# Modulated 1D convolutions (four layers, one core): the blurred taps of layer 1 are made before layer 0's first products

## The reference, cut to what matters

```python
def _layer(x, style, w, b, mw, mb, typ):
    s = style @ mw.T + mb
    weight = SCALE * w * s[:, None, :, None]
    demod = lax.rsqrt(jnp.sum(weight * weight, axis=(2, 3)) + EPS)
    weight = weight * demod[:, :, None, None]
    if typ == 'same':
        out = jax.vmap(_conv_same)(x, weight) + b[None, :, None]
    elif typ == 'upsample':
        out = jax.vmap(_conv_up)(x, weight.transpose(0, 2, 1, 3)) + b[None, :, None]
        out = _blur(out, 2.0 * blur_k, (1, 1))
    elif typ == 'downsample':
        xb = _blur(x, blur_k, (2, 2))
        out = jax.vmap(_conv_down)(xb, weight) + b[None, :, None]
    return out
out = x
for i, typ in enumerate(('same', 'upsample', 'same', 'downsample')):
    out = _layer(out, style, weights[i], biases[i], mod_w[i], mod_b[i], typ)
x = x + out
```

## Time and profile before

| | before |
|---|---|
| median of 3 runs | 181.14 us (180.51 to 181.2) |
| the profiled execution | 181.34 us, span in the trace 179.2 us |
| granted TensorE clock, mean over the span | 0.98 |
| PE (matmul) busy | 170.8 us, 95% |
| VectorE busy | 125.4 us, 70% |
| ScalarE busy | 57.2 us, 32% |
| GpSimd busy | 15.4 us, 9% |
| chain that ended last | PE 91%, DVE 3%, issue 2%, ACT 1% |

### The profile page before, as it was taken

The page is one execution under the profiler, slowest core; times in us unless marked ns, Lnnn a source line. Parts: engine busy times, 40 slices in busy tenths (PEclk is TensorE's granted clock), DMA queues, the critical chain, the costliest instruction groups (busy, mean ns, idle before and its releaser), DMA issues.

```text
span 179.2 us, 7986 instructions
## 1 busy us (share of the span) xinstructions
PE 170.8 (95%) x3567; PEld 155.4 (87%) x3567; DVE 125.4 (70%) x265; ACT 57.2 (32%) x126; POOL 15.4 (9%) x47
## 2 busy tenths in 40 slices
PE   7899999999999799999999999999999999999990
PEld 5598969986677498999999999999999999998960
DVE  7659755896776946758494949494949394958793
ACT  3433554122142233324151514243332424222110
POOL 7002202800001300200000000000000000000000
PEclk9958999999999999999999999999999999999999
DMA  4960003033000986827274645456463637333322
GB/s 135 365 75 2 4 0 91 4 89 123 0 5 4 273 278 240 225 88 222 98 170 161 159 166 152 177 115 214 103 224 91 237 89 236 93 121 75 140 117 117
DMA packets 11778, 23.65 MB, mean 132 GB/s; under 512 B 5184, under 2 KB 5728, under 8 KB 11744
## 3 DMA queue, kind: packets, MB, share of 16 engines
q1 hardware_dynamic: 11680, 23.12, 42.8%
q10 hardware_dynamic: 64, 0.02, 0.1%
HBM read 8.85 MB, written 8.39 MB: 96 GB/s over the span
## 4 chain that ended last, share of the span: by engine, by line
PE 91%; DVE 3%; issue 2%; ACT 1%; DVEq 0%
PE p_m L415 26%; PE p_le L354 14%; PE p_lo L354 13%; PE p_le L398 12%; PE p_m L433 11%; PE p_lo L385 5%; PE p_le L304 2%; PE p_m L294 1%; PE p_le L402 1%; PE p_m L512 1%; PE p_m L505 1%; DVE r_sb L769 1%; PE p_m L285 1%; PE p_m L343 1%; PE p_m L495 1%
## 5 line engine op out<-in xcount | busy, mean ns | idle before, releaser
L415 PE MATMUL p_m<-u,Hw 64*64 64x256 f32 x896 | 61.0, 377 | 0.3 <-DVE z_sb L787 0.3
L415 PEld LDWEIGHTS p_m<-u,Hw 64*64 64x64 f32 x896 | 46.9, 132 | 2.6 <-issue 0.5
L354 PE MATMUL p_lo<-xin,w0s 64*64 64x259 f32 x384 | 31.0, 406 | 0.0
L736 DVE SCALAR_TENSOR_TENSOR Hw<-p_le,pvec,Hw 128x320 f32<-128x320 f32 x16 | 8.8, 551 | 31.0 <-ACT Hw L605 31.0
L354 PE MATMUL p_le<-xin,w0s 64*64 64x260 f32 x384 | 30.1, 407 | 0.2 <-DVE Hw L743 0.2
L398 PE MATMUL p_le<-R_sb,F_st 64*64 64x192 f32 x320 | 30.0, 324 | 0.0
L398 PEld LDWEIGHTS p_le<-R_sb,F_st 64*64 64x64 f32 x320 | 25.8, 133 | 1.1 <-issue 0.4
L354 PEld LDWEIGHTS p_lo<-xin,w0s 64*64 64x64 f32 x384 | 21.8, 137 | 2.4 <-issue 0.3
L354 PEld LDWEIGHTS p_le<-xin,w0s 64*64 64x64 f32 x384 | 20.7, 137 | 3.4 <-issue 1.1
L605 ACT ACTIVATE Hw<-p_le,pvec 128x448 f32<-128x448 f32 x16 | 10.2, 635 | 37.0 <-PE p_le L398 37.0
L787 DVE SCALAR_TENSOR_TENSOR z_sb<-p_m,pvec,s_sb 128x512 f32<-128x512 f32 (+1 forms) x30 | 21.0, 742 | 0.9 <-PE p_m L415 0.9
(11 more groups left out here) (122 smaller groups left out, 155.9 us busy)
## 6 DMA issues: line engine op xcount, KB each, us to landing
xin<-in_x_dram SPq DMA_DIRECT2D x16, 512.0 KB, 4.8
out_dram<-ot SPq DMA_DIRECT2D x16, 512.0 KB, 5.4
Hw<-Hw SPq DMA_DIRECT2D x30, 192.0 KB, 3.0
wn<-in_L_cond_weights_dram SPq DMA_DIRECT2D x1, 192.0 KB, 3.5
mwn<-in_L_cond_mod_w_dram SPq DMA_DIRECT2D x1, 128.0 KB, 2.3
xe<-in_x_dram SPq DMA_DIRECT2D x2, 56.0 KB, 8.2
cn<-in_cond_dram ACTq DMA_DIRECT2D x1, 16.0 KB, 2.1
bn<-in_L_cond_mod_b_dram ACTq DMA_DIRECT2D x1, 1.0 KB
```

The lines of the kernel that those rows point to most:

```text
L354: ins = pe.matmul(bank[h * C:(h + 1) * C, s, 0:n], w0s[p % 2][rows, k, :], xin[p % NX][rows, i0:i0 + 2 * n - 1:2], start=(k == 0), stop=(k ...
L415: ins = pe.matmul(bank(h)[s * C:(s + 1) * C], tap(p, h, s, blk), u[p % 2][h * C:(h + 1) * C, s, j, k:k + NM], start=(k == 0), stop=(k == l ...
```

## The change

The taps are no longer made after `compose_R(0)`. The two matmuls of k = 0 are issued on TensorE ahead of the demodulation products, the four of k = 1 and 2 right behind them, both ahead of layer 0 of pair 0. They now go to `p_le[:, 0]` instead of `p_m2[:, 1]`. Since layer 0's even products write to the same bank, these wait until ScalarE has copied the taps out. ScalarE makes that copy ahead of `evac_odd(0)` instead of behind `evac_R(0)`. Where the taps stood, TensorE now waits for the copy `G_mv` and for `dt_` before layer 2's taps.

```diff
-            def blurred_taps(l, bank, cid, n):
+            def blurred_taps(l, bank, cid, n, taps=range(K)):
-                for k in range(K):
+                for k in taps:
                     for h in range(2):
...
             ins.then_inc(put["GT"], 1)
 
+            pe.wait_ge(made["cid"], 1)
+            blurred_taps(1, p_le[:, 0], cid2, NF, (0,))
+
             pe.wait_ge(copied["wsumT"], 1)
             pe.wait_ge(made["style2"], 1)
...
             ins.then_inc(put["demod"], 1)
+            blurred_taps(1, p_le[:, 0], cid2, NF, (1, 2)).then_inc(put["FT"], 1)
...
             layer0_odd(0)
+            pe.wait_ge(copied["F_st"], 1)
             layer0(0, p_le, NE, 0, le_done)
             pe.wait_ge(copied["V_st"], 1)
             compose_R(0)
 
-            pe.wait_ge(made["cid"], 1)
+            pe.wait_ge(copied["G_mv"], 1)
             pe.wait_ge(made["dt"], 1)
-            blurred_taps(1, p_m2[:, 1], cid2, NF).then_inc(put["FT"], 1)
             taps_transposed(2, b_m13[0], 256).then_inc(put["w2T"], 1)
...
             act.activation(dq[:], dt_[:], ACT.Sqrt).then_inc(sqrt_done, 1)
+            act.wait_ge(put["FT"], 1)
+            act.activation(F_st[:], p_le[:, 0, 0:NF * C].rearrange("p (a c) -> p a c", c=C), ACT.Copy,
+                           scale=1.0 / 32).then_inc(copied["F_st"], 1)
             evac_odd(0)
...
             evac_R(0)
-            act.wait_ge(put["FT"], 1)
-            act.activation(F_st[:], p_m2[:, 1, 0:NF * C].rearrange("p (a c) -> p a c", c=C), ACT.Copy,
-                           scale=1.0 / 32).then_inc(copied["F_st"], 1)
             make_A(1)
```

## The result

| | before | changed |
|---|---|---|
| first series, median of 6 executions each | 181.15 us (180.51 to 181.25) | 183.14 us (181.17 to 183.22) |
| ratio, with 95% interval | | 1.0079 (1.0043 to 1.0115) |
| second series, median | 181.63 us (31 executions) | 181.99 us (10), ratio 1.0023 (0.9985 to 1.006) |
| profiled execution | 181.34 us, span 179.2 | 181.17 us, span 179.0 |

The change made the kernel slower in the first series, and by an amount that can't be told from nothing in the second. The places at which TensorE's granted clock falls and rises differ from one execution to the next (in four traces of the changed kernel the rise lies between 14.6 and about 16.5), and the time follows them. Over all 18 executions of the change the median is 182.26 us and 8 are at 182.6 or more. Of 90 of the kernel before one is at 182.6 or more, and three more are at 182.51 to 182.53.

A forecast was written before the change was run, and what follows sets the result against it. TensorE's work was taken as the bound (busy 95%), with 1.01 us of VectorE slack in the prologue. An earlier clock rise gains 0.95 to 1.05 us, less 0.1 for later tight spots: 0.9, so 180.3 us, range 179.9 to 181.7.

The forecast's parts named there:

- Which t: Prologue, TensorE: long matmuls from 8.43 us bring the clock's rise, t, earlier; gain 0.9 us, chance 0.45.
- before 13 us: Sign of a right forecast: TensorE's granted clock in the prologue rises before 13 us.
- 8.98 + t/2: Layer 0 of pair 0, TensorE: its end in us, t being the clock's rise; 16.54 for t = 15.12.
- t unchanged: Prologue, clock rise still at 15.12 us: `make_diffs(0)` starts at 16.65, 1.25 late; H(1) 0.1 late.
- cap by VectorE: VectorE needs 4.50 us from `make_diffs(0)` to the sum of H(0)'s taps; gain capped at 0.95 to 1.05.
- A: Rival, chance 0.38: prologue clock rises where it did, VectorE takes TensorE's gain; 181.2 us, range 180.9 to 181.5.
- B: Rival, chance 0.13: prologue clock rises later, at 17.6 us, as taps may not count like layer 0's matmuls; 182.6 us.
- C: Rival, chance 0.04: prologue clock does not stay down at 8.30 us or comes back at once; 179.7 us.
- forecast 0.36, bounds 0.2 and 0.5: Demodulation products on TensorE, behind the two early taps matmuls: late by 0.36 us, moving `dt_` from 10.19 to 10.55.
- The wait of layer 0's even products for `F_st`: TensorE, layer 0: costs nothing, as the odd products hide the 0.44 us copy; uncovered it would be 0.7 us.
- GpSimd's start does not move: `xse` beside VectorE's `pvec` instructions: starts unchanged, so part of VectorE's 0.36 us delay is absorbed; 0.2 taken.

The follow-up runs named there:

- filled kernel: The change with a dummy matmul on the other 64 array rows beside each taps matmul: medians 180.14 us (ratio 0.9944) and 180.91 us (0.9973).
- third alone: Kernel before with only the two k = 0 taps matmuls moved ahead of the demodulation products: median 180.90 us, ratio 0.9966.
- none ahead: The change with all six taps matmuls behind the demodulation products: median 183.09 us, ratio 1.0081 against the kernel before.

## Why the prediction was wrong, point by point

Forecast was 180.3 us, faster by 0.5%; measured was 183.14 in the first series, outside of 179.9 to 181.7, and slower.

**The step that failed is "Which t".** I took the taps for long matmuls like layer 0's, and concluded from "long matmuls (320 columns) from 8.43 on" that the clock would rise earlier. It did not: the low stretch stayed 6.8 us long in three traces of the change with a fall, with rises at 14.6, 15.2 and 16.3, and in the one without a fall the low rate lasted until about 16.5; "before 13 us" was forecast. What the text had as a point for rivals, that the taps use 64 of 128 rows, is what the filled kernel points to: with the other rows busy beside them the stretch was 3.4 us. I had named that reason and weighed it as a detail. Nothing in between was seen either: of the ten traces with a fall ahead of layer 0's end, seven have a low stretch of 6.8 us and three one of 3.4.

**What hangs on t was right.** The rule for layer 0's end, 8.98 + t/2, can be held against the traces: for rises at 14.6, 16.3 and 11.8 (filled) it gives 16.3, 17.1 and 14.9, and the ends were 16.22, 17.16 and 14.97. The change's second trace has the rise at 15.18, nearly the 15.12 of the case "t unchanged": `make_diffs(0)` starts at 16.65 as forecast, and H(1) at 22.52, where 22.55 was forecast. The cap by VectorE was right as well: the sum starts 4.43 us behind `make_diffs(0)`, forecast was 4.50. From there the time follows, if VectorE has no idle time before the sum:

| trace | make_diffs(0) | idle before the sum | span | span less make_diffs(0) |
|---|---|---|---|---|
| before | 15.40 | 1.01 | 179.2 | 163.8 |
| before, no fall of the clock | 15.93 | 0.25 | 179.0 | 163.1 |
| third alone | 15.27 | 0.50 | 178.5 | 163.2 |
| change | 16.29 | 0 | 179.0 | 162.7 |
| change, second series | 16.65 | 0 | 179.6 | 163.0 |
| change, fall at 9.5 | 17.24 | 0 | 180.0 | 162.8 |
| change, long execution | 18.00 | 0 | 180.6 | 162.6 |
| none ahead | 17.67 | 0 | 180.3 | 162.6 |
| change, without warm-up | 16.32 | 0 | 179.3 | 163.0 |
| change, filled | 15.05 | 0 | 177.9 | 162.9 |
| change, filled, second trace | 15.54 | 0 | 178.7 | 163.2 |

Where VectorE has no slack the last column is the same within 0.6 us, for starts of `make_diffs(0)` from 15.05 to 18.00. An early rise would have given what I said: the filled kernel, with its rise at 11.8, took 180.09 us in its profiled execution.

**The rivals.** A (0.38) gave 181.2 and is what the short executions show, with a wait of H(1) of 0.25 us (0.4 forecast). Its time was a little low: the profiled execution of 181.17 us had its rise at 14.6, half a microsecond ahead of A's; the one with the rise at 15.18 took 181.77, above A's 181.5. B (0.13) gave 182.6 for a rise that comes later. It describes the long ones in size, 182.7 to 183.2, but that is partly luck: I had put it down to a rise at 17.6 behind a fall at 8.3. In the long execution no fall is recorded, the rise comes at about 16.5, and the demodulation products were 1.4 us late (10.77 against 9.35). C was not seen.

**The range was built on one trace.** Three of the four times that I had were at 181.14 to 181.34 and one was at 180.51. I read that as noise of the measurement. It is the clock's edges falling elsewhere. By the mean granted clock, over the series:

| mean clock of the execution | kernel before (84 executions) | change (18) |
|---|---|---|
| 0.977 to 0.981, as in the traces with a low stretch of 6.8 us | 48, median 181.65 | 10, median 181.86 |
| 0.985 or 0.986, too high for that; traces with 3.4 us have 0.984 to 0.987 | 9, from 180.44 to 180.72 | none |
| 0.995 to 1.0, as in the traces without a fall at the start | 27, median 181.28 | 8, median 183.16 |

Executions without a fall are not much more frequent in the change. They cost 1.9 us more in it, and the others 0.2 more, near A's price. This is where the first series' 183.14 comes from: four of its six have a mean clock of 1.0, and the prediction had no case for an execution without a fall. The two traces say why it is dear. In the kernel before the rise near 13.4 let layer 0 end at 14.98, and `make_diffs(0)`, at 15.93, still waited for VectorE's own row; in the change the rise near 16.5 let layer 0 end at 17.8, and `make_diffs(0)` starts at 18.00. No trace of the kernel before with a clock of 0.985 was taken. The point "t unchanged at 15.12" should have been a case over many t.

**Small terms.** From the end of the sums' copy to `dt_` it took 1.41 us (8.79 to 10.20) instead of 1.16, a delay of 0.25; forecast 0.36, bounds 0.2 and 0.5. The wait of layer 0's even products for `F_st` cost nothing in any trace: in the first trace the copy ended at 12.82, and the first record of the even products is at 13.93. "GpSimd's start does not move" was wrong by 0.13 us: `xse` started at 13.79 instead of 13.66. The two `pvec` instructions beside it took 1.23 us and ended at 15.03, `xse` at 15.00. The Trainium skill has it that two such operations hold one port pair in turn (page "SBUF — State Buffer", section "SBUF: two separate sides"), and the two ends agree. `dt_` started at 10.20, 0.01 later than before, so that this trace doesn't test how much of a delay is absorbed; it was hidden behind layer 0 anyway, with 0.98 us of idle time ahead of `make_diffs(0)`.

What stays open: how often each place of the edges occurs, since it differs between series (4 of 6 long executions, then 3 of 10), and what the filled kernel's four executions at 181.6 to 181.8 look like, of which no trace was taken (their mean clock speaks for no fall). That the fill works by the rows in use, and not by the mere number of matmuls, was not tried apart.

## What to carry to other kernels

Moving work into a hole gains the hole at most. Ask also which engine's start is pushed back by what now stands ahead of it: here four matmuls ahead of layer 0 used up another engine's 1.01 us of slack, and in executions whose clock stayed low until layer 0 the whole change cost 1.9 us. Do not count on any long matmul to bring the clock back: the taps, on half of the array's rows, left the low stretch at 6.8 us, and with a dummy on the idle half beside each it was 3.4 us, at no cost. Take several traces before building on the place of a clock edge, and sort the executions by their mean granted clock before comparing medians.

## What the runs showed of the hardware

The places of the clock's edges are not the program's alone: in traces of the same changed kernel the fall stood at 7.8, 8.4, 9.5, or was absent, with the rise at 14.6, 15.2, 16.3 and about 16.5. Taking the warm-up out of the kernel before did not make it slower (ratio 0.9978, 0.995 to 1.0007). And a trace without a recorded fall shows a granted clock of 1.00 from the start even where TensorE runs at 1.2 GHz, as 1.06 us for L321's products instead of 0.66 shows: the duration of a known matmul is the better witness.
